# An intra-chunk solve on TensorE in 64x64 products, with the old state's product moved between them

## The reference

```
h = layernorm(x) * (1 + ca) + sa                  # ca, sa, ga ... from silu(c) @ wmod
v = h @ Ww.T;  rk = h per head / its norm;  wk = rk one token later
per chunk of 64 tokens and head (4 heads of 64):
    A0    = -strict_lower(wk wk^T * L)            # L: powers of the head's decay
    A     = inv(I - A0)                           # 64x64, unit lower triangular
    v_new = A @ (v - wk @ S)
    o     = (rk * decay) @ S + strict_lower(rk wk^T * L) @ v_new
    S     = decay^64 * S + (wk * tail)^T @ v_new
x = x + ga * (h + (alpha * o) @ Wr.T)
x = x + gb * ffn(layernorm(x) * (1 + cb) + sb)    # 256 -> 1024 (silu gate) -> 1024 -> 1024 -> 256
```

## Time and profile before

| | |
|---|---|
| median of 3 runs | 1798.08 us |
| the profiled execution | 1797.14 us, span 1795.3 us |
| TensorE matmul (PE) busy | 1742.7 us, 97% |
| VectorE busy | 1143.2 us, 64% |
| ScalarE busy | 987.9 us, 55% |
| GpSimd busy | 592.9 us, 33% |
| chain that ended last | PE 93%, VectorE 2%, DMA 1%, issue 1%, ScalarE 1% |
| DMA | 24 GB/s on average, 289 GB/s in the first fortieth |

### The profile page before, as it was taken

How to read it: one execution, slowest core, us unless ns; L and a number is a source line. 1 busy time by engine, 2 the same in 40 slices (tenths; PEclk the granted TensorE clock), 3 DMA queues, 4 the chain that set the end, 5 groups by cost and what they waited for, 6 DMA issues and landing times.

```text
span 1795.3 us, 62791 instructions
## 1 busy us (share of the span) xinstructions
PE 1742.7 (97%) x26614; PEld 1682.8 (94%) x26614; DVE 1143.2 (64%) x3075; ACT 987.9 (55%) x2281; POOL 592.9 (33%) x693
## 2 busy tenths in 40 slices
PE   5699999999999999999999999999999999999999
PEld 3688999999999999999999999999999999999998
DVE  6676766666666666666666666666666666666432
ACT  4564555555654555554555555555555555555554
POOL 3443332432432332332332332342333243233111
PEclk7699999999999999999999999999999999999999
DMA  8200000000000000000000000000000000000000
GB/s 289 65 14 20 20 20 14 21 16 12 20 20 20 14 20 9 20 19 18 17 20 8 20 20 20 14 20 8 20 20 19 14 20 8 20 20 14 8 2 13
DMA packets 33028, 43.79 MB, mean 24 GB/s; under 512 B 8356, under 2 KB 24872, under 8 KB 32744
## 3 DMA queue, kind: packets, MB, share of 16 engines
q1 hardware_dynamic: 30608, 37.06, 7.1%
q10 hardware_dynamic: 2136, 2.65, 0.5%
HBM read 22.78 MB, written 8.39 MB: 17 GB/s over the span
## 4 chain that ended last, share of the span: by engine, by line
PE 93%; DVE 2%; DMA 1%; issue 1%; ACT 1%; POOL 0%; ACTq 0%; SPq 0%; DVEq 0%; POOLq 0%
PE mlp L1154 63%; PE mlp L1224 6%; PE solo L1154 3%; PE duo L1419 3%; PE solo L1289 3%; PE solo L1137 2%; PE duo L1408 1%; PE duo L1340 1%; PE duo L1125 1%; PE solo L1142 1%; PE solo L1428 1%; PE duo L1121 1%; PE duo L1310 1%; DMA w_raw<-in_wts 1%; PE duo L1410 1%
## 5 line engine op out<-in xcount | busy, mean ns | idle before, releaser
L1154 PE MATMUL mlp<-act_hi,w_hi 128*128 128x256 f32 x4096 | 989.7, 284 | 5.4 <-DVE full L1015 2.1
L1154 PE MATMUL mlp<-act_lo,w_hi 128*128 128x256 f32 x4096 | 968.0, 279 | 0.0
L1154 PEld LDWEIGHTS mlp<-act_hi,w_hi 128*128 128x128 f32 x4096 | 769.0, 188 | 14.2 <-DVE full L1015 2.6
L1154 PEld LDWEIGHTS mlp<-act_lo,w_hi 128*128 128x128 f32 x4096 | 769.5, 188 | 0.8
L803 ACT ACTIVATE full<-mlp,scale_sb 128x256 f32<-128x256 f32 x512 | 245.1, 479 | 529.0 <-PE mlp L1154 528.2
L890 DVE TENSOR_TENSOR act_lo<-full,act_hi 128x256 fp32r<-128x256 f32 x512 | 251.5, 491 | 353.3 <-ACT act_hi L804 352.2
L665 POOL TENSOR_TENSOR act_lo<-full,act_hi 128x256 fp32r<-128x256 f32 x256 | 186.2, 733 | 503.5 <-ACT act_hi L793 503.5
L804 ACT ACTIVATE act_hi<-mlp,scale_sb 128x256 fp32r<-128x256 f32 x512 | 241.4, 471 | 0.0
L1154 PE MATMUL mlp<-xh,w_hi 128*128 128x256 f32 x768 | 189.5, 285 | 5.3 <-DVE xl L1009 4.1
L1154 PE MATMUL mlp<-xl,w_hi 128*128 128x256 f32 x768 | 188.7, 283 | 0.0
L604 POOL TENSOR_TENSOR rstd<-ve,minus_half 128x2 f32<-128x2 f32 x64 | 48.8, 762 | 367.1 <-DVE ve L842 367.1
(11 more groups left out here) (177 smaller groups left out, 2673.7 us busy)
## 6 DMA issues: line engine op xcount, KB each, us to landing
w_raw<-in_wts SPq DMA_DIRECT2D x22, 512.0 KB, 5.7
kg<-r SPq DMA_DIRECT2D x64, 126.0 KB
xin<-in_x SPq DMA_DIRECT2D x62, 128.0 KB
out_y<-y SPq DMA_DIRECT2D x62, 128.0 KB, 2.5
wmod_sb<-in_wmod ACTq DMA_DIRECT2D x1, 1024.0 KB, 8.7
kg<-last SPq DMA_DIRECT2D x64, 2.0 KB
last<-r SPq DMA_DIRECT2D x64, 2.0 KB, 1.7
wmod_sb<-in_wmod ACTq DMA_DIRECT2D x1, 512.0 KB, 5.3
```

The costliest lines, as they stand in the source:

```text
L1154: mm = pe.matmul(dst, *general_ops, start=is_first and i == 0, stop=is_last and i == 1)
```

## The change

1. `first_term` takes `cross` (its mask is transposed now) as the stationary operand over a whole half, 64x64, against `inv` itself, 32 columns. It writes the transposed link, and no transpose of `inv` is waited for. 32 products of 32x32 per chunk become 16. In the steady part the product of half c goes to the other half's partitions, `half(1 - c)`. The links behind it carry the transposed chain: `square_and_term` is as before, and `n` 3 brings the result back to the right half.
2. The identity is added to the square (`CO_UNIT`), so that `n` 3 gives the finished transposed inverse in PSUM, from where ScalarE writes `diag`. VectorE's addition and transpose after `n` 3 go; one addition of 128x256 in `first_part` comes.
3. `inner` and `own` are 64x64 products for all blocks (32 and 64 columns); `own` has 16 instead of 18 products. `own_full` is evacuated by one copy of 128 partitions instead of two of 32.
4. The old state's product (`old_state`, 16 products) leaves `inter` after `l3` 1 and stands in `lead` (and `solve` 0), two products of it behind each two of `own`. It writes bank `duo[1]`. `own` and `inner` use the array tiles from a half to itself, `old_state` and `first_term` those from a half to the other one. ScalarE's copy to `o_state` goes to a new entry `old` after `l2` 0; GpSimd's decay of the state goes to `lead`, ahead of `far` and `stats`.
5. The transposed `inv` of the next chunk must be swapped between the halves. SyncE does it by two DMAs of 64x256 (`move_inverse`), and TensorE waits for them ahead of `l2` 2.
6. `wr_sb` and its load of 256 KB go: all four sequences use `wr_turned`, since all outputs have the heads swapped now.

```diff
-    c[:, CO_MASK + C:CO_MASK + 2 * C] = (j // HB == i // HB) & (j // SB > i // SB)
+    c[:, CO_MASK + C:CO_MASK + 2 * C] = (j // HB == i // HB) & (j // SB < i // SB)
...
-        ("l3", 1): [("values", 0, 1), ("pred", 0, 0), ("gram", 0, 1), ("inter", 0, 0), ("turn", 0, 0), ("intra", 0, 1), ("u", 0, 0)],
+        ("l3", 1): [("values", 0, 1), ("pred", 0, 0), ("gram", 0, 1), ("turn", 0, 0), ("intra", 0, 1), ("u", 0, 0)],
...
+            def move_inverse(a):
+                sp.wait_ge(inv_t_ready, a + 1)
+                for c in range(2):
+                    sp.dma_start(first_inv_t[half(1 - c)], square_t[half(c)]).then_inc(inv_moved, 16)
...
-                    if name == "inter":
+                    if (name == "lead" or name == "solve" and k == 0) and items is not alone:
                         pool.wait_ge(inter_full, a)
...
-                for i in range(2):
-                    ins = act.activation(diag[:, :, HB * i:HB * (i + 1)], inv8_t[:], ACT.Copy, scale=con[:, CO_BLK + i:CO_BLK + i + 1])
+                for i in range(2):
+                    ins = act.activation(diag[:, :, HB * i:HB * (i + 1)], of_head(duo[1][:, 1, 0:2 * NP * HB]), ACT.Copy, scale=con[:, CO_BLK + i:CO_BLK + i + 1])
...
-                dve.transpose(square_t[:].rearrange("p k n -> p (k n)"), duo[1][:, 0, 0:2 * NP * HB]).then_inc(square_ready, 1)
-                dve.tensor_tensor(first_two[:], inv, of_head(duo[1][:, 0, 2 * NP * HB:4 * NP * HB]), ALU.subtract).then_inc(first_ready, 1)
+                dve.transpose(square_t[:].rearrange("p k n -> p (k n)"), duo[1][:, 0, 0:2 * NP * HB]).then_inc(square_turned, 1)
+                dve.tensor_tensor(first_two[:], first_inv_t, of_head(duo[1][:, 0, 2 * NP * HB:4 * NP * HB]), ALU.subtract).then_inc(first_ready, 1)
+                dve.wait_ge(square_turned, a + 1)
+                dve.tensor_tensor(square_t[:], square_t[:], con[:, CO_UNIT:CO_UNIT + HB].unsqueeze(1).to_broadcast([P, 2 * NP, HB]),
+                                  ALU.add).then_inc(square_ready, 1)
...
-                    if name == "n" and k == 3:
-                        dve.wait_ge(rest_full, now)
-                        dve.tensor_tensor(inv, first_two[:], of_head(duo[1][:, 1, 0:2 * NP * HB]), ALU.add).then_inc(inv_ready[1], 1)
-                        dve.wait_ge(inv_ready[1], now)
-                        dve.transpose(inv8_t[:].rearrange("p k n -> p (k n)"), inv.rearrange("p k n -> p (k n)")).then_inc(inv_t_ready[1], 1)
...
-                return pe.matmul(of_head(duo[0][rows, 0, 0:2 * NP * HB])[:, m, :], inv8_t[rows, m, :], cross[rows, e, q, HB * i:HB * (i + 1)], start=True, stop=True)
+                return pe.matmul(of_head(duo[0][half(to), 0, 0:2 * NP * HB])[:, m, :], cross[half(c), m // NP, m % NP, :], inv[half(c), m, :], start=True, stop=True)
...
+            def old_state(b, hp, c, e):
+                q, col = b * (H // 2) + hp, NP * DH + (2 * hp + c) * C
+                return pe.matmul(duo[1][half(1 - e), b, col:col + C], state[half(e), q, c, :], rg[half(e), q, c, :], start=True, stop=True)
...
+                        for m in range(2 * NP):
                             for c in range(2):
-                                own(p, m, m // NP, m % NP, half(c), slice(0, C), False)
+                                last_own = own(p, m, c)
+                            b, hp, chain = m // NP, m // 2 % 2, m % 2
+                            for e in range(2) if items is not alone else ():
+                                last_old = old_state(b, hp, chain, e)
...
+                        for m in range(2 * NP):
+                            for c in range(2):
+                                last_inner = inner(m, c)
+                            for c in range(2) if with_next else ():
+                                last_first = first_term(m, c, 1 - c)
```

More of the change, by code:

```diff
@@ L131, in main @@
     wv_sb = sb("wv_sb", [KT, D])
-    wr_sb = sb("wr_sb", [KT, D])
     wr_turned = sb("wr_turned", [KT, D])
@@ L216, in main @@
     step_and_inv = sb("step_and_inv", [2, 2 * NP, HB])
-    step_n, inv = (step_and_inv[:, i] for i in range(2))
-    inv8_t = sb("inv8_t", [2 * NP, HB])
+    step_n, first_inv_t = (step_and_inv[:, i] for i in range(2))
+    inv = sb("inv", [2 * NP, HB])
     diag = sb("diag", [2 * NP, C])
@@ L297, in main @@
         ("l1", 7): [("lead", 0, 0), ("far", 0, 1), ("stats", 0, 2)],
-        ("l2", 0): [("norm", 0, 2)],
+        ("l2", 0): [("old", 0, 0), ("norm", 0, 2)],
         ("l2", 1): [("keys", 0, 0)],
@@ L555, in step @@
                         attention(n + 1, 1 - g)
+                    if items is mixed and (whole or n + 1 < STEPS):
+                        move_inverse(n + 1)
                     if not whole and n == STEPS + 1:
@@ L903, in part @@
                     if name == "wr":
[L904 to L908 removed]
+                        dve.wait_ge(small_in, 5 * 16)
+                        for hp in range(NPAIR):
+                            a = NPAIR + H + hp
+                            ins = dve.tensor_scalar(wr_turned[:, hp, :], wr_turned[:, hp, :], gam[:, a:a + 1], None, ALU.mult)
                         ins.then_inc(wr_ready, 1)
@@ L1189, in layer @@
                             weights_in(m, unit[name, k])
+                        if items is mixed and name == "l2" and k == 2 and (not isinstance(n, int) or n + 1 < STEPS):
+                            pe.wait_ge(inv_moved, 32 * n - 64)
                         if items is second:
@@ L1312, in part @@
                         mm.then_inc(pred_full, 1)
-                    if name == "inter":
-                        pe.wait_ge(const_in, 16)
-                        pe.wait_ge(rg_ready, a)
-                        pe.wait_ge(pred_full, a)
-                        for b, hp, c, e in turns:
-                            q, col = b * (H // 2) + hp, NP * DH + (2 * hp + c) * C
-                            mm = pe.matmul(duo[0][half(e ^ b), b, col:col + C], state[half(e), q, c, :], rg[half(e), q, c, :], start=True, stop=True)
-                        mm.then_inc(inter_full, 1)
                     if name == "n":
@@ L1332, in part @@
                             pe.wait_ge(first_ready, now)
-                        for e, q, c, i in quarters:
+                        for m in range(2 * NP) if k == 1 else ():
+                            for c in range(2):
+                                mm = first_term(m, c, c)
+                        for e, q, c, i in quarters if k > 1 else ():
                             rows, m = quarter(c, i), e * NP + q
-                            if k == 1:
-                                mm = first_term(m, e, q, c, i)
                             if k == 2:
@@ L1339, in part @@
                             if k == 3:
-                                mm = pe.matmul(of_head(duo[1][rows, 1, 0:2 * NP * HB])[:, m, :], square_t[rows, m, :], first_two[rows, m, :], start=True, stop=True)
+                                back = quarter(1 - c if items is mixed else c, i)
+                                mm = pe.matmul(of_head(duo[1][back, 1, 0:2 * NP * HB])[:, m, :], square_t[rows, m, :], first_two[rows, m, :], start=True, stop=True)
                         mm.then_inc({1: step_full, 2: first_full, 3: rest_full}[k], 1)
@@ L1407, in part @@
                         for q, c, e in blocks:
-                            pe.matmul(duo[0][half(e ^ pair_of[q][0]), c, q * C:(q + 1) * C], vn[half(c), q, e, :], intra[p][half(c), e, q, :], start=True, stop=True)
+                            pe.matmul(duo[0][half(1 - e), c, q * C:(q + 1) * C], vn[half(c), q, e, :], intra[p][half(c), e, q, :], start=True, stop=True)
                         for q, c, e in blocks:
@@ L1418, in part @@
                             for hp in range(H // 2):
-                                mm = pe.matmul(duo[1][:, 0, b * D:(b + 1) * D], o_state[:, b * (H // 2) + hp, :], (wr_sb, wr_turned)[b][:, hp, :],
+                                mm = pe.matmul(duo[1][:, 0, b * D:(b + 1) * D], o_state[:, b * (H // 2) + hp, :], wr_turned[:, hp, :],
                                                start=hp == 0, stop=hp == H // 2 - 1)
```

117 lines of the change are left out of this document (52 added, 65 removed), and 1 row of the table third.

## The result

The changed kernel takes 1750.91 us (median of 4 runs, 1749.67 to 1752.09); the kernel before took 1799.25 us beside it (1797.32 to 1801.52). The ratio is 0.9731, with a 95% interval from 0.9714 to 0.9748: some 48 us off, where 17.3 were forecast, and outside the range of 1770 to 1790. The profiled execution took 1752.09 us with a span of 1750.3; before it was 1797.14 and 1795.3, so 45.0 us are to be found in the two traces.

What follows compares the result with a forecast made beforehand. TensorE, busy 97% of the span, was taken as the bound. Terms 13.6 + 3.4 - 0.7 + 1.0 = 17.3 us off 1798.1 gave 1780.8 us; own range 1775 to 1786, 8 in 10 from 1770 to 1790.

Steps and rivals of the forecast that it cites:

- Part 6: At the start: dropping the 256 KB load of `wr_sb` saves 0.9 us of DMA time, half of it counted, 0.5 us.
- The old state's product: Moved from after `l3` 1 to free tiles in `lead`: costs nothing there, gains 0.47 us a step, 13.6 us.
- Rival 1: In `lead`: streamed columns alone decide, 0.036 us per instruction, `lead` 1.89 us; 1772.1 us in all, chance 0.22.
- A `lead` without a next chunk: In steps 31 and 1: 1.83 us before, 2.18 after, a loss of 0.35 us each, together 0.7.
- Rival 3: In `lead`: tiles of two row halves writing one bank exclude each other, 4.04 us; 1836.6 us, chance 0.07 with rival 4.
- Rival 4: In `lead`: old products don't find their tiles free, 0.98 us more a step; 1809.2 us, chance 0.07 with rival 3.
- rival 2: In each step: a new wait of about 0.5 us behind GpSimd's decay or the swap; 1795.3 us, chance 0.09.
- the opening: At the start: first link's shorter wait and the dropped load together gain 1.0 us, bounds 0 and 3.
- The first link's wait: In step 1: the first link waits for `inv` alone, no longer for its transpose, 0.5 us gained.

Runs made afterwards that it cites:

- e2: The changed kernel plus an unused tensor of 1920 bytes that puts every tensor behind it back where it lay in the kernel before: 1774.5 us, ratio 0.9869.
- h2: The changed kernel with `act_hi` and `act_lo` 64 bytes higher in each partition, everything else at its place: 1802.01 us, ratio 1.0043.
- e1: The kernel before with `wr_sb` allocated last and constants 32 columns longer, so tensors behind them lie 1920 bytes lower: 1785.88 us, ratio 0.9925.
- e3: The changed kernel with the old state's product back behind `gram`, its copy and decay with it, all places kept: 1775.49 us, ratio 0.9872.
- g2: The changed kernel with the first link of chunks 0, 1 and 2 waiting for the transpose of `inv` again: 1754.84 us, ratio 0.9767.
- g1: The changed kernel with the 256 KB load of `wr_sb` put back into unused room, read by nothing: 1752.33 us, ratio 0.9757.

## Why the prediction missed

**The step that failed** is the sum's silence on the wide matmuls. Part 6, "the load of `wr_sb`, 256 KB, goes", was priced as a load alone. That it and the wider constants move every tensor behind them was not in the sum, not in the range and in none of the rivals. It is worth 20.9 us in the steady stretch (in the median 22.53 to 22.17 us in the wide run ahead of `lead`, 5.62 to 5.45 behind it, and less in the others), and 23.6 us by the medians of e2 and the changed kernel. e2 and h2 show that it is the places: with work and order the same, the pace changes with them. e1 adds that the places don't do it alone: with the old work they give 12.2 us. The new work by itself gives the wide matmuls nothing (e2), but at the new places it holds the fast pace, which the old work does in half of the steps. Why it does is open. The gain was luck: 64 bytes further it is a loss, 27.5 us between h2 and e2.

**Right, by its own steps.** The old state's product is free in `lead` (0.02 us by e3) and 0.46 us leave the values' stage. `lead` is 2.20 us against 2.18: `inner` and `first_term` take 2.20 - 0.21 - 0.98 - 0.11 = 0.90 us, 0.056 per instruction, where 0.055 came from the stationary columns. Rival 1 (0.036) is out. A `lead` without a next chunk takes 2.19 (1663.47 to 1665.66) against 1.83 in the earlier trace rows, a loss of 0.36 as summed. In the stretch of 28 steps the sum had 28 x (0.47 + 0.12) = 16.5 us for the small stages, the traces 14.7. `lead` gives the difference: its median fell from 2.29 to 2.21, but its mean only from 2.36 to 2.34, since some `lead`s have a gap of 0.2 to 1.1 us that the trace puts down to "issue". Both kernels have them, e3 has none, and their cause stays open.

**Rival 3 is out by the row.** `own`, `old_state`, `inner` and `first_term` write, each from both row halves, into one bank in turn, and the stage takes 2.20 us, not 4.04. The rule of the Trainium skill (TensorEngine Tiling (Array Packing), Restrictions and Gotchas) would have it slower; the measurement decides, and no exclusion is seen here. Rival 4 is out by e3, and rival 2 by the windows: PE is busy 52.00 of 52.00 us. So VectorE's addition, the copy `old`, GpSimd's decay and the two DMAs cost nothing, as priced. The page's row of the two DMAs (56 in all, 64 KB each, us to landing):

```profile
step_and_inv<-square_t SPq DMA_DIRECT2D x56, 64.0 KB, 2.0
```

They land after 2.0 us, where over 12 were free.

**A second term was too small:** the opening, 1.0 us in the sum with bounds of 0 and 3. Up to the first steady `lead`, whose last wide matmul ahead starts at 213.2 us before and 204.4 after, the change gave 8.8. The sum had 1.1 for this stretch: the opening's 1.0, one stage of 0.47 after `l3` 1, less 0.35 for step 1. The new work alone gives 7.9 (e2, 205.3), the places alone 4.2 (e1, 209.0); the two overlap. The first link's wait was priced at 0.5 and is worth some 3 (g2); the load was priced at 0.5 and is worth nothing by then (g1). Of the 7.9, 3.5 stand already at the first wide matmul (70.50 us before, 67.04 in e2), and what makes them was not told apart. With 7.9 in place of 1.1 the sum is 24.1 us without a move of the tensors, and e2 has 1798.1 - 1774.5 = 23.6.

## What to carry to other kernels

When a change adds or removes a tensor, compare the places of all that the busiest engine reads, before and after, and price the move; where no trace shows that price, it belongs into the range. Test an edit at unchanged places (an unused tensor of the same size does it), or a gain of the allocation is booked to the idea. And read a pipelined engine by the distance of starts over a counted stretch: the mean duration moved by 2 ns of 284 here, the pace by 4.3 of 117.7.

## What the hardware showed

- The pace of back-to-back matmuls of 128x256 depends on the places of their operands mod 256 bytes: 0.1133 us with both streamed halves at 64, up to 0.1233 for 32 with 64, at a granted clock of 1.00 in the rows shown. 0.1133 us is 272 cycles of 2.4 GHz for 256 columns, and none of the places tried was faster. The weights stood at 128 in all kernels, so their place as the stationary operand was not varied. `y`, where the activations are stationary and the weights streamed, changed its pace all the same when the activations moved (h2).
- At 64 mod 256 there are two stable paces, 0.1133 and 0.1178, which hold for a whole stretch, and the kernel before shows both at 192 too. e1 changes between them from step to step, with the same instructions each time. What chooses was not found.
- Two sets of 64x64 products on disjoint tile pairs overlap completely, though each set writes one bank from both row halves: 64 instructions in 0.98 us, where 32 on two tiles alone take 0.93.
